# Two graph layers on one core: rows 16 apart, a catch-up in five rounds, and later stores of two pairs of kept words

## What is computed

```python
# layer 0
a = adj.astype(x.dtype); deg = jnp.sum(a, axis=1, keepdims=True)
x1 = a @ x / deg
x = _layernorm(x + jnp.concatenate([x1, x], axis=1) @ weight + bias)
# layer 1
h = x @ W.T
e = (h @ a1)[:, None] + (h @ a2)[None, :]
e = jnp.where(adj == 0, -inf, e)
x = _layernorm(x + softmax(e, axis=1) @ h)
```

## Time and profile before

| | us |
|---|---|
| median of 3 runs | 1012.5 |
| lowest and highest | 1010.69 and 1013.55 |
| the profiled execution | 1011.9 |
| its span, first to last instruction | 1010.2 |
| PE busy | 970.8 |
| DVE busy | 732.5 |
| ACT busy | 601.8 |
| POOL busy | 277.1 |

### The profile page before, as it was taken

One profiled execution on the slowest core, in us unless ns is written; L12 is line 12 of the kernel. 1 busy time (PEld: TensorE's weight loads), 2 busy tenths in 40 slices (PEclk: granted clock), 3 DMA queues, 4 the chain that ended last, 5 costly groups with the idle time before them and its releaser, 6 DMA issues.

```text
span 1010.2 us, 22065 instructions
## 1 busy us (share of the span) xinstructions
PE 970.8 (96%) x8727; PEld 866.9 (86%) x8727; DVE 732.5 (73%) x1791; ACT 601.8 (60%) x604; POOL 277.1 (27%) x275
## 2 busy tenths in 40 slices
PE   6899889999999998999999999999999999999996
PEld 6899767888988897888898888888888888888885
DVE  3698887888877786778777676666654986677674
ACT  3988898888878887988868676767421000000000
POOL 4345544333435433434333333332000000000000
PEclk9999989999998999999999999999999999999999
DMA  9999999999999999999999999999421022222101
GB/s 283 394 420 420 421 420 421 419 421 421 421 421 417 420 418 422 415 419 414 410 392 362 420 344 349 341 350 311 159 77 71 22 84 86 90 90 89 34 24 34
DMA packets 50490, 301.70 MB, mean 299 GB/s; under 512 B 6608, under 2 KB 7888, under 8 KB 17360
## 3 DMA queue, kind: packets, MB, share of 16 engines
q0 software_dynamic: 37344, 270.03, 66.9%
q1 hardware_dynamic: 12336, 29.47, 8.7%
q10 hardware_dynamic: 704, 0.75, 0.3%
HBM read 286.46 MB, written 13.76 MB: 297 GB/s over the span
## 4 chain that ended last, share of the span: by engine, by line
PE 61%; DMA 27%; ACT 7%; issue 3%; DVE 2%; POOL 0%; ACTq 0%; DVEq 0%
PE ps_agg L403 33%; DMA adj_in<-in_adj_dram,chunk 26%; PE ps_part L403 22%; ACT edges L585 5%; PE ps_y L403 4%; PE ps_h L752 1%; ACT parts L576 1%; PE ps_h L707 0%; DMA x_all<-in_x_dram 0%; DVE parts L911 0%; PE ps_x1T L745 0%; POOL adj_in L1399 0%; DVE packed L963 0%; DVE edgesT L948 0%; PE ps_y L707 0%
## 5 line engine op out<-in xcount | busy, mean ns | idle before, releaser
L403 PE MATMUL ps_agg<-parts,edgesT 128*128 128x255 f16 (+1 forms) x5240 | 592.3, 274 | 20.3 <-DVE edgesT L948 18.9
L403 PEld LDWEIGHTS ps_agg<-parts,edgesT 128*128 128x128 fp8e4 x5240 | 514.2, 98 | 85.7 <-DVE edgesT L948 24.2
L585 ACT ACTIVATE edges<-adj_in 128x2048 fp8e4<-128x2048 int32 x256 | 481.2, 1905 | 62.8 <-DMA adj_in<-in_adj_dram,chunk 61.2
L1399 POOL DMA_INDIRECT adj_in<-in_adj_dram,chunk x256 | 272.2, 1063 | 430.4 <-ACT edges L585 419.7
L948 DVE STREAM_TRANSPOSE edgesT<-edges 128x512 uint32<-128x512 uint32 x256 | 167.1, 691 | 60.2 <-ACT edges L585 59.6
L403 PE MATMUL ps_part<-parts,edgesT 128*128 128x256 f16 x1664 | 190.2, 273 | 0.3 <-DVE parts L1050 0.3
L403 PEld LDWEIGHTS ps_part<-parts,edgesT 128*128 128x128 fp8e4 x1664 | 162.8, 98 | 18.8 <-DVE parts L1050 0.5
L652 ACT ACTIVATE std<-mean_var,eps 128x1 f32<-128x1 f32 x64 | 18.9, 295 | 226.4 <-DVE mean_var L1224 226.4
L963 DVE SCALAR_TENSOR_TENSOR packed<-edgesT,packed 128x2048 uint32<-128x2048 uint32 x48 | 109.6, 2283 | 1.2 <-DVE packed L959 0.5
L403 PE MATMUL ps_part<-parts,packed 128*128 128x256 f16 x772 | 87.2, 273 | 0.0
L403 PEld LDWEIGHTS ps_part<-parts,packed 128*128 128x128 fp8e4 x772 | 75.6, 98 | 8.7
(11 more groups left out here) (125 smaller groups left out, 655.3 us busy)
## 6 DMA issues: line engine op xcount, KB each, us to landing
adj_in<-in_adj_dram,chunk POOLq DMA_INDIRECT x256
adj_in<-partial_sums SPq DMA_DIRECT2D x16, 256.0 KB, 5.7
out_dram<-edges SPq DMA_DIRECT2D x60, 64.0 KB, 3.3
partial_sums<-partial SPq DMA_DIRECT2D x13, 256.0 KB
packed_adj<-parts SPq DMA_DIRECT2D x2, 1024.0 KB
adj_in<-packed_adj SPq DMA_DIRECT2D x2, 832.0 KB, 5.1
x_all<-in_x_dram POOLq DMA_DIRECT2D x6, 256.0 KB, 13.1
x_all<-in_x_dram SPq DMA_DIRECT2D x6, 256.0 KB, 14.8
```

The lines of the kernel that those rows point to most:

```text
L403: done = eng.matmul(bank[:, 0:cols], rows[:, n // BYTES, n % BYTES, :], moving[:, n, :], start=(n == first), stop=(n == last))
L585: act.activation(edges[:, r // 2, r % 2, :], adj_in[:, m % SLOTS, :], ACT.Copy, scale=EDGE[t % GROUP], saturate=False).then_inc(s_conv, 1)
L1399: pool.indirect_dma_start(adj_in[:, m % SLOTS, :], None, adj_chunks, bass.IndirectOffsetOnAxis(chunk[:, 0:1], 0), element_offset=first_row ...
```

## The change

Three things are changed.

- **Rows 16 apart.** The 128 partitions of a load of adj hold 32 rows, 4 pieces of 8 KB each. These rows were 8 apart (RUN = 8) and are 16 apart. x comes in runs of 16 rows, 8 KB, where it came in runs of 8 rows, 4 KB. The first words of x are 4 rows a partition instead of 8, so that the second group of transposes (j = 1) waits for the rest of the first quarter. The DVE transposes read each 32 words with a step of 4 words (16 bytes) instead of 2.
- **Five rounds.** The groups are caught up with in five rounds instead of three. A round is (group, first band, bands, first tile, tiles of the group in each tile): group 0 takes bands 0 and 1 in tiles 12 and 13, group 1 the same in 14 and 15, group 2 three bands in tiles 16 to 19, group 0 two more in 20 to 23, group 1 three more in 24 to 27. CAUGHT goes from 2, 3, 4 bands to 4, 5, 3. There are two banks of PSUM for it. The two later rounds of groups 0 and 1 are stored apart and added in the second stage.
- **Later stores.** The words of pair 1 and pair 0 are stored after the partial sums of groups 8 and 12, not 7 and 11.

```diff
-    CATCH = 12
-    CAUGHT = [2, 3, 4]
-    CTILES = GROUP * len(CAUGHT)
-    CWORDS = P * max(CAUGHT)
+    ROUNDS = [(0, 0, 2, 12, 2), (1, 0, 2, 14, 2), (2, 0, 3, 16, 1), (0, 2, 2, 20, 1), (1, 2, 3, 24, 1)]
+    CAUGHT = [max(first + bands for g, first, bands, at, by in ROUNDS if g == k) for k in range(FIRST_INLINE)]
+    CWORDS = P * max(bands for g, first, bands, at, by in ROUNDS)
+    SECOND = [k for k in range(len(ROUNDS)) if ROUNDS[k][1] > 0]
...
-    RUN = 2 * BYTES
-    x_quarters = x.rearrange("(a s b w c) f -> s a w b (c f)", a=NQ, s=QUARTERS, b=NBLK // QUARTERS // RUN, w=QUAD, c=RUN)
-    out_halves = out.rearrange("(a g w h c) f -> g h a w c f", a=NQ, w=QUAD, h=2, c=BYTES)
+    STEP = 4
+    RUN = STEP * BYTES
+    x_quarters = x.rearrange("(a s w c) f -> s a w (c f)", a=NQ, s=QUARTERS, w=QUAD, c=RUN)
+    out_steps = out.rearrange("(a g w h c) f -> g h a w c f", a=NQ, w=QUAD, h=STEP, c=BYTES)
...
             def store_caught(k):
                 sp.wait_ge(s_ckept, GROUP * (k + 1))
-                sp.dma_start(part_dram[k], c_part[:, :, :].rearrange("p c f -> p (c f)")).then_inc(s_cst, 16)
+                wait(sp, s_cst, 16 * k)
+                sp.dma_start(part_dram[round_home(k)], c_part[:, :, :].rearrange("p c f -> p (c f)")).then_inc(s_cst, 16)
+            def kept_at(k):
+                g, first, bands, at, by = ROUNDS[k]
+                return at + (GROUP - 1) // by + 1
             for g in range(GROUPS - 1):
+                for k in range(len(ROUNDS)):
+                    if GROUP * g < kept_at(k) < GROUP * (g + 1):
+                        store_caught(k)
...
-                    if g == KEEP_UNTIL[n] - 1:
+                    if g == KEEP_UNTIL[n]:
                         store_words(n)
-                if 0 <= g - CATCH // GROUP < len(CAUGHT):
-                    store_caught(g - CATCH // GROUP)
+                for k in range(len(ROUNDS)):
+                    if kept_at(k) == GROUP * (g + 1):
+                        store_caught(k)
...
             def weighted_hi(g):
                 act.wait_ge(s_wh, g + 1)
                 if GROUP * g == CBLOCK:
-                    act.wait_ge(s_cst, 16 * len(CAUGHT))
+                    act.wait_ge(s_cst, 16 * len(ROUNDS))
...
             def transpose_x(j):
-                if j < RUN // BYTES:
+                if j == 0:
                     pe.wait_ge(s_xfirst, 16 * NQ)
...
-                src = edges[:, r // 2, r % 2, :].bitcast(u32).rearrange("p (g q h) -> p g h q", q=QUAD, h=2)
+                src = edges[:, r // 2, r % 2, :].bitcast(u32).rearrange("p (g q h) -> p g h q", q=QUAD, h=STEP)
...
                 if joins:
                     check(t // GROUP - 1, 1)
                     join(t // (2 * GROUP) - 1)
+                for i, k, c in caught_at(t):
+                    unpack_caught(i, k, c)
+                for i, k, c in caught_at(t - 1):
+                    keep_caught(i, k)
...
+                for i, k in enumerate(SECOND):
+                    if c == 0 and g == ROUNDS[k][0]:
+                        dve.wait_ge(s_partld2[i], 16)
+                        dve.tensor_tensor(part_in[:, s, :], part_in[:, s, :], part_in[:, 5 + i, :], ALU.add)\
+                            .then_inc(s_pjoin, 1)
+                        dve.wait_ge(s_pjoin, i + 1)
```

More of the change, by code:

```diff
@@ L53, in bass_two_graph_layers, with caught_at @@
     EARLY = FIRST_INLINE * GROUP
-    CATCH = 12
-    CAUGHT = [2, 3, 4]
-    CTILES = GROUP * len(CAUGHT)
-    CWORDS = P * max(CAUGHT)
+    ROUNDS = [(0, 0, 2, 12, 2), (1, 0, 2, 14, 2), (2, 0, 3, 16, 1), (0, 2, 2, 20, 1), (1, 2, 3, 24, 1)]
+    CAUGHT = [max(first + bands for g, first, bands, at, by in ROUNDS if g == k) for k in range(FIRST_INLINE)]
+    CWORDS = P * max(bands for g, first, bands, at, by in ROUNDS)
+    SECOND = [k for k in range(len(ROUNDS)) if ROUNDS[k][1] > 0]
+    def caught_at(t):
+        return [(GROUP * k + c, k, c) for k, (g, first, bands, at, by) in enumerate(ROUNDS) for c in range(GROUP)
+                if t == at + c // by]
     def bands_of(g):
@@ L328, in bass_two_graph_layers @@
         s_partld = [sem(f"partial_landed{s}") for s in range(5)]
+        s_partld2 = [sem(f"partial_of_second_round_landed{g}") for g in range(len(SECOND))]
+        s_pjoin = sem("rounds_added")
         s_unp = sem("unpacked")
@@ L761, in second_layer_inline, with caught @@
                     .then_inc(s_part, 1)
-            def caught(i):
-                blocks = GROUP * CAUGHT[i // GROUP]
+            def caught(i, k):
+                g, first, bands, at, by = ROUNDS[k]
+                blocks = range(GROUP * bands)
                 if i == 0:
@@ L767, in caught @@
                 pe.wait_ge(s_cunp, i + 1)
-                wait(pe, s_ckept, i)
-                contract(pe, ps_caught, c_words[:, i % 2, :], weighted_rows, range(blocks), 0, blocks - 1).then_inc(s_csum, 1)
+                wait(pe, s_ckept, i - 1)
+                contract(pe, ps_caught[i % 2], c_words[:, i % 2, :], weighted_rows[:, GROUP * first:NBLK, :],
+                         blocks, 0, blocks[-1]).then_inc(s_csum, 1)
             def second_layer(u, blocks):
@@ L786, in _ @@
                     second_layer_inline(t)
-                if catching(t):
-                    caught(t - CATCH)
+                for i, k, c in caught_at(t):
+                    caught(i, k)
                 if t == 7:
@@ L1142, in one_tile, with unpack_caught, keep_caught @@
                                          ALU.logical_shift_left if up > 0 else ALU.logical_shift_right, ALU.bitwise_and)
-            def unpack_caught(i):
-                k, c = i // GROUP, i % GROUP
-                words = slice(0, P * CAUGHT[k])
+            def unpack_caught(i, k, c):
+                g, first, bands, at, by = ROUNDS[k]
+                source = words_of_pair[store_of(g)][:, P * first:P * (first + bands)]
                 if c == 0:
-                    dve.wait_ge(s_joined, store_of(k) + 1)
+                    dve.wait_ge(s_joined, store_of(g) + 1)
                 wait(dve, s_csum, i - 1)
-                one_tile(c_words[:, i % 2, words], words_of_pair[store_of(k)][:, words], k, c).then_inc(s_cunp, 1)
-            def keep_caught(i):
+                one_tile(c_words[:, i % 2, 0:P * bands], source, g, c).then_inc(s_cunp, 1)
+            def keep_caught(i, k):
                 dve.wait_ge(s_csum, i + 1)
```

39 lines of the change are left out of this document (18 added, 21 removed).

## The result

The changed kernel takes **1024.57 us** (1023.74 to 1025.44, 4 runs) against 1011.6 us before (1010.58 to 1013.55, 4 runs): ratio 1.0122, 95% interval 1.0109 to 1.0135. It is 1.2% slower. The profiled execution took 1023.74 us, with a span of 1022.1.

A forecast was written before the change was run, and what follows sets the result against it. The prediction took loads of adj as the bound up to tile 35 and PE after it. 1011.9 - 5.2 (matmuls moved) + 10.6 (tile 35 later, mainly the wait at tile 28) + 1.5 (start) = 1018.8 us, range 1007 to 1028.

The forecast's parts named there:

- The transposes: DVE transposes of adj: reading at a 16-byte step instead of 8 was taken to cost 0.
- The rival: DVE transposes: 16-byte step halves the pace, 0.57 us more each, DVE becomes the bound, +20 to 1039 us; chance 0.14.
- DVE's work in the rounds: Tiles 12 to 27: DVE keeps and unpacks eight more small tiles, covered by 12% to spare, cost nothing.
- The wait at tile 28: ACT's weighted_hi(5) waits for the last caught store, making tile 29 8.2 us late on PE.
- The clock loss after the gap, +2.9: PE after the idle gap in tile 28: a lower granted clock adds 2.9 us, with 0 as the other end.
- P itself: Time at which PE begins tile 28: forecast 328.7 us, 325.50 before.
- Matmuls moved, -5.2: Second stage, where PE is the bound: 48 matmuls at 0.109 us leave it, 5.2 us saved.
- The start, +1.5: Kernel start: group 1's x rows arrive later, delaying the first dense and adj loads, +1.5 us, ends -1 to +6.
- Later stores, -1.2, at most 1 back: Loads alone would let tile 35 begin 1.2 us earlier; the later store at tiles 37 and 38 costs at most 1.
- Loads slower: Loads of adj: rows 512 KB apart cost 3% of the load rate, 9 us more, 1028 us; chance 0.08.

The follow-up runs named there:

- e3: Changed kernel with its transposes reading every second word (8 bytes) instead of every fourth, loads and x as changed: 1013.45 us.
- e7: Kernel before plus 15 DVE instructions at its end, reading 512 words at steps of 4 to 32 bytes: transposes 0.67 us at 8 bytes, 1.04 at 16.
- e2: Changed kernel with rows 8 apart and x as before, keeping five rounds, later stores and the wait at tile 28: 1012.83 us.
- e1: Kernel before with only the rows 16 apart layout (adj, x, first words, 16-byte transposes, output), three rounds and old stores: 1015.2 us.
- e4: Changed kernel with caught sums in the start weights' buffer and unpacked words 4 blocks later, so nothing waits at tile 28: 1016.95 us.
- e5: Changed kernel with rows 8 apart and buffers moved as in e4, keeping five rounds and later stores: 1007.58 us.
- e8: e5 with ACT issuing the load of w0 ahead of the first words of x: 1005.69 us.
- e6: e5 with the words of pairs 1 and 0 stored four tiles earlier, as before the change: 1008.74 us.
- e9: e8 with the words of pairs 1 and 0 stored four tiles earlier, as before the change: 1007.68 us.

## Why the prediction was right in sign and nearly in size, and partly for the wrong reason

The time came out 13 us over before, 6 over my number and inside the range. But the sum is made of other pieces than I wrote, and that it came as near as 6 us is in part luck: two errors of opposite sign.

- **The transposes: the step that failed.** "If nothing changes, the cost is 0, which I take, since 8 bytes cost nothing against 4." They take 1096 ns instead of 691, and this is the largest piece: 11.1 us (e3). The inference from 4 and 8 bytes to 16 was wrong, since the price starts between 8 and 16 (e7). The rival's condition held, at 0.14 I gave it too little. Its price was too high: 0.40 us each instead of 0.57, and 11 us instead of 20, because DVE with 0.40 us more is only just fuller than the loads allow. (The 20 was loosely made as well: 11 us a tile against 10.0 by the loads is 1.0 us over, not 0.7.) The Trainium skill ("SBUF — State Buffer", section "Door 1: The DMA port swizzle") speaks of 16-byte lines and of at least two accesses to each; the runs agree with it (0.67 us at 8 bytes, 1.04 at 16, 1.05 at 32), and it should have weighed more than an extrapolation from two points on one side of the line. The same note has 4 fp32 as how far one can stride for free. That is not so here: a step of 4 words takes 1.04 us and one of 3 already 0.81, and the measurement decides.
- **DVE's work in the rounds: "nothing".** True with rows 8 apart: tiles 12 to 27 take 170.0 us in e2, 169.8 before. Not true once the transposes are slow: the cover of 12% that I named is gone, and the same tiles take 175.6 us. DVE is busy there for 139.7 us before, 144.5 in e2, 162.8 in e1 (which takes 168.3 us) and 169.3 in the changed kernel: once the layout has filled it, the 5 to 6.5 us of DVE work that the rounds bring cost 7.3 us of time. Layout alone +3 us (e1), rounds and stores alone +0.6 (e2), both together +13: the costs do not add, since each used up the slack of the other. From tile 29 to 35 in the changed kernel DVE is busy 59.11 of 61.27 us and PE all of it, so there the two cost no more than PE.
- **The wait at tile 28: mechanism and size right.** Forecast and measured after P, the start of tile 28: store issued +3.5 and +3.56; landing 8 and 6.7 us; ACT's weighted_hi +11.5 and +10.2; tile 29 +18.1 and +17.3. Taken away it gives back 7.6 us (e4), where 8.2 was the forecast, or 5.3 us with fast transposes (e5 against e2). There the loads bound tiles 34 and 38 next: e5 takes 12.3 us from tile 33 to 34 and 12.1 from 37 to 38, where e2 takes 10.4 and 10.8. A part of the wait comes from a detail of the change: the two instructions that keep a caught sum stood ahead of the check in a step and now stand behind it. Ahead of the check's 1.22 us the store would be issued about 1.2 us sooner, by my estimate; no run tried it.
- **The clock loss after the gap, +2.9: there, but smaller, and not on the path.** In the changed kernel the granted clock is 0.65 of full between 349.79 and 353.90 us, thus partly at the lower level of 1.2 GHz, and the 24 matmuls behind the gap take 4.19 us where the same 24 of the next tile take 2.78: 1.4 us lost. In e2 the clock is 0.55 there and they take 4.93 us, 2.2 lost. But tile 29 waits for something else. Its conversions and transposes stand behind weighted_hi, the last transposes end at 355.35, and PE, done with the 24 and one more small one, idles 1.32 us once again. In e2 too the transposes release tile 29. Its own 64 matmuls take their normal 7.16 us in both. The forecast put the loss behind the start of tile 29; on the path it is 0. The transposes of tile 29 and the 24 matmuls of the tile after the gap, in the changed kernel:

```profile
351.11 4.24 DVE L971 STREAM_TRANSPOSE edgesT<-edges 128x512 uint32<-128x512 uint32 x4
...
362.62 2.78 PE L413 MATMUL ps_part<-parts,edgesT 128*128 128x256 f16 x24
```

- **P itself.** Forecast 328.7, measured 338.1. Without slow transposes it is 327.0 (e3) or 326.1 (e2). The forecast carried over tile 26's slow clock of the earlier trace rows (12.44 + 9.50 us, and 2.6 for the added blocks, = 24.5); e2 needs 21.6 us for tiles 26 and 27, that is 10.8 a tile at full clock. 2.9 us too much, a gap's cost taken from one execution of another order of work.
- **Matmuls moved, -5.2:** the rest of the kernel from tile 35 on is 4.7 us shorter, 4.9 in e2. Right.
- **The start, +1.5:** not borne out as a cost of x. The first dense is at 13.33 against 12.84, tile 0 at 42.98 against 41.25. But e3, with the same loads of x, has them at 12.82 and 41.64, and e2, with the old ones, at 13.23 and 41.70. The kernels with slow transposes have tile 0 at 42.32 to 43.38, so most of the 1.7 us seems to go with the step. Group 1 waited for its quarter as said:

```profile
3.74 1.12 PE L721 MATMUL ps_catT<-ident,x_all 128*128 128x128 f32 x4 [0.47 <-DMA x_all<-in_x_dram]
...
12.42 1.12 PE L721 MATMUL ps_x1T<-ident,x_all 128*128 128x128 f32 x4 [5.86 <-DMA x_all<-in_x_dram]
13.33 1.92 PE L728 MATMUL ps_y<-w_agg,x_all 128*128 128x128 f32 x8
```

  These are PE's rows of the changed kernel. Its w0 was there by 6.38 us, so only x held it, and w0 did not land later in proportion, as the upper end of this term had it.
- **Later stores, -1.2, at most 1 back:** 1.3 to 1.5 us are given back at tile 38 (e5, e8), and what is left from tile 31 to 39 is a gain of 0.6 to 0.8 us. In the changed kernel neither shows, since from tile 29 on PE is busy without a gap.
- **Loads slower: no.** 421 GB/s in the windows above, and e3 within 0.6 us of e2. The Trainium skill's rule on a row pitch of 512 KB ("DMA: Bandwidth & Descriptors", section "Latency and other measured facts") does not show in loads of 8 KB pieces from memory into SBUF.

By the runs the sum is 1011.6 + 0.6 (rounds, stores and wait, e2) + 0.6 (loads and start, e3 against e2) + 11.1 (step of the transposes, e3) = 1023.9, measured 1024.57; what is left is the difference of the comparisons' own before (1011.6 and 1012.2). Each term is a difference of neighbours in a row, so the sum has to come out and is no proof by itself; in another order the shares are others (the layout costs 3 us alone and 9.4 us with the rounds but without the wait, e4 against e5). My two errors, 0 for the transposes and some 6 us too much for the clock (2.9 in P, 2.9 behind the gap), partly cancelled.

## What to carry to other kernels

A cost that is flat at two points need not be flat at the third: measure an access step, in a few instructions behind the kernel's end, before a whole layout rests on it. An engine with 12% to spare covers one new cost, not two; ask of each part what it costs once the others have taken the slack. When a buffer is shared with a later user, look at who stores its last contents, in which step, and how far ahead of the reuse: here one tile of work in between decides 5 to 8 us, and a buffer that is dead by then (the first weights) removes it.

## What the runs showed of the hardware that was not expected

- A 32-bit word read every 16 bytes costs DVE some 50% more than one every 4 or 8 bytes, in transposes (1.04 against 0.67 us for 512 words a partition), copies (0.61 against 0.42) and ANDs (0.61 against 0.42); 12 bytes lie between, 32 bytes cost the same as 16.
- The load of w0 (128 KB) reached DVE at very different times behind the first words of x in its queue: at 7.72 to 12.44 us where these are 8 rows a partition (12.11 before, 12.44 in e2, 10.93 in e5, 7.72 in e6; e5 and e6 have the same code there), at 5.62 to 8.62 us where they are 4 rows (e1, the changed kernel, e3, e4). Ahead of them it came at 4.06 and 4.36 (e8, e9), and the first words were on PE at 7.62 and 7.22 instead of 4.91 in e5. Why it varies was not settled.
- The granted clock fell after waits of PE, but the length of the gap alone does not tell the loss. 2.93 us of idle time went with 2.9 us lost over 64 matmuls (tile 26 before), 2.29 us with 1.7 (tile 34 of e9), 4.27 us with 1.4 over 24 matmuls (changed kernel), 6.33 us with 2.2 over 24 (e2). The same 1.36 us ahead of tile 0 went with 1.7 us lost in e3 and none in e2. Where the next tile waits for another engine, as in the changed kernel and e2, the loss costs nothing.
